# Query weights in one set of chunks, converted with the key weights in slots 9 to 12 of the last unit of a head group

## The chip, the cores and the metric

One core of a Trainium2 chip runs the whole program. The metric is the device time of one execution in microseconds (us). A difference of about 0.3% (8 us here) is what a measurement of this kernel can tell from none.

## What is computed

A decoder layer on x of 16 sequences x 256 tokens x 512 features, in float32. The change touches only the first of its three parts, the self-attention with 16 heads of size 128:

```python
q = split_heads(hidden_states @ wq)
k = split_heads(hidden_states @ wk)
v = split_heads(hidden_states @ wv)
...
q = _apply_rotary(q, cos, sin)
k = _apply_rotary(k, cos, sin)
...
attn = jnp.einsum('bhqd,bhkd->bhqk', q, k) * scale
attn = jnp.where(valid, attn, neg)
attn = jax.nn.softmax(attn, axis=-1)
out = jnp.einsum('bhqk,bhkd->bhqd', attn, v)
...
return out @ wo
```

After it come a cross-attention with a context and a mixture of experts.

## The kernel before

**Units and slots.** The 16 heads are four head groups of four heads (g = 0 to 3), and the 16 sequences are eight pairs. A unit u is one pair in one group: 32 units, u = 8g + pair, one after the other. A unit has 16 slots (the code's `s`; k is `s % SLOTS`), and in each slot TensorE does one projection of 12 matmuls of 128x512. The table `FRAME` says which: in slots 0 to 3 the values (V) of the unit, in 4 and 8 the queries (Q) of its heads 2 and 3, in 5 and 9 the keys (K) of its heads 2 and 3, in 6, 7, 10 and 11 the output projection (O) of the unit before, and in 12 to 15 Q0, K0, Q1, K1 of the next unit. Even slots begin with the scores of a head (lines 572 to 575), odd slots with the transposes of probabilities (583) and their product with V (594, 595). Every engine runs the same slots in its own program order; only semaphores hold one for another.

**Weights in two parts.** A weight chunk is 128x512 of float32; each of Q, K, V and O has four chunks per group. Each chunk is loaded by SyncE's DMA queue into one of four buffers `raw` (`load_raw`, line 274), rounded by ScalarE to `whi` (`w_round`, 728), and the rest, raw less whi, is taken by GpSimd into `wlo` (`w_rest`, 442). A projection of a kind waits until all four chunks of that kind are there (`weights_at`, a count on the semaphore `s_wlo`). `sequence` numbers the chunks; chunk i may be loaded only when chunk i - 4 has been through GpSimd (`s_wlo` at i - 3). `converted(s)` says which chunks go through in slot s, and SyncE, ScalarE and GpSimd all read it in their own loops over s. `last_use` is what `w_round` waits for before it writes over a chunk of the group before.

**The change of head group.** It falls into units 7, 15 and 23, called here changes 1, 2 and 3. There, before: Q chunks of the next group in slots 0 to 3, V chunks in 4 to 7, K chunks two and two in slots 10 and 11. Q has two sets of chunks (0 to 3 and 16 to 19), so its new weights can be written while the old are in use. The first user of the new Q weights is the projection in slot 12, of the new K weights the one in slot 13.

**SyncE's queue in such a unit.** In program order: the loads of `converted(s)`; at slot 10 also `load_xn(u + 2)` (line 260: two DMAs of 1024 KB, the normalised input of two units on), which waits until the K projection of slot 9 is done; at slot 12 the store and the load of the residual rows (291, 286).

**ScalarE in slots 10 to 13 of such a unit**: the exponentials of step 5 (`exps`, 709), the roundings of that slot (728), `pt_evac` (716), the roundings of slot 11, two `o_round` (722), the exponentials of slot 12, `pt_evac`. VectorE takes the row maxima (871) in slot 12 only after the rest of the first rounded output (`o_rest`, 885), and the product with V in slot 13 (594) waits for that rest too. GpSimd adds the two halves of the rotary turn (`turn_add`, 435) one slot after each Q or K projection, ahead of the `w_rest` of its slot.

Of the kernel before, what the change touches and what calls it, by code (L numbers as in the profile page):

```python
# [6 lines left out]
F32R = mybir.dt.float32r  # L7
# [6 lines left out]
P = 128  # L14
B, L, D = 16, 256, 512
TILES = B * L // P
TB = L // P
CB = D // P
# [4 lines left out]
NCH = 3 * CB + HG  # L23
# [9 lines left out]
CH_Q, CH_K, CH_V, CH_O = 0, CB, 2 * CB, 3 * CB  # L33


def attention_stages(nc, x, w_all, rope, xt, x1, ctx_in, ctx_t, gamma, sq, sk, mv2, mv3, x2, x2_at, cst):
# [4 lines left out]
    with ctx:  # L41
# [38 lines left out]
        def at(name, shape, dt, kb):  # L80
            return nc.alloc_sbuf_tensor_at(name, shape, dt, offset=area + int(kb * KB))
# [25 lines left out]
        var2 = at("var2", [P, TILES], F32, 27.5)  # L107
        seed2 = at("seed2", [P, TILES], I32, 27.75)
        half2 = at("half2", [P, TILES], F32, 28)
        STACK_AT = (0, CH_V, CH_K)  # L110
        qst = [at(f"qst{i}", [P, XPT, D], F32R, 60.5 + 2 * STACK_AT[i]) for i in range(STACKS)]
        kst = [at(f"kst{i}", [P, XPT, D], F32R, 100.5 + 2 * STACK_AT[i]) for i in range(STACKS)]
        qp = [at(f"qp{i}", [P, 2, D], F32R, 60.5 + 2 * NCH + 4 * i) for i in range(2)]
        kp = [at(f"kp{i}", [P, 2, D], F32R, 100.5 + 2 * NCH + 4 * i) for i in range(2)]
        RING_AT = (60.5 + 2 * CH_O, 100.5 + 2 * CH_O, 28.5, 36.5, 44.5, 52.5)
        xprt = [at(f"xprt{i}", [P, XPT, D], F32, RING_AT[i]) for i in range(RING)]

# [45 lines left out]
        PAIRS = B // 2  # L163
# [8 lines left out]
        at, turned, number, place, order = {}, {}, {}, {}, []  # L172
# [10 lines left out]
        for s in range(FIRST, LAST):  # L183
            kind, ahead, i = FRAME[s % SLOTS]
# [7 lines left out]

        def sequence(g, kind, c):

            return NCH * g + 4 * ("QVKO" if g else "QKVO").index(kind) + c

        def weights_at(g, kind):

            return sequence(g, kind, 3) + 1

        def chunk_of(g, kind, c):

            if kind == "Q":
                return (16 if g % 2 else 0) + c
            return {"K": CH_K, "V": CH_V, "O": CH_O}[kind] + c

        def converted(s):

            f, k = s // SLOTS, s % SLOTS
            g = (f + 1) // PAIRS  # L210
            if f % PAIRS == PAIRS - 1 and 0 < g < G:
                if k < 4:
                    return [(g, "Q", k)]
                if k < 8:
                    return [(g, "V", k - 4)]
                if k in (10, 11):
                    return [(g, "K", 2 * (k - 10) + i) for i in range(2)]
            g = f // PAIRS
            if f % PAIRS == 0 and 0 <= g < G and k >= 12:
                return [(g, "O", k - 12)]  # L220
            return []
# [2 lines left out]

        def last_use(g, kind):

            if kind == "Q":
                return number["K", PAIRS * (g - 1) - 1, 3] if g > 1 else 0
            u = PAIRS * g - 1
            return number[kind, u, 3] + 1 if g else 0  # L230

# [24 lines left out]
        def _(sp):  # L256
# [10 lines left out]
            def load_raw(g, kind, c):  # L267
                i = sequence(g, kind, c)
                if i >= 4:
                    sp.wait_ge(s_wlo, i - 3)  # L270
                if i in (3 * CB, NCH):
                    sp.wait_ge(s_nrm, 8 if i < NCH else 4 * PAIRS)
                src = w_all[g, {"Q": CH_Q, "K": CH_K, "V": CH_V, "O": CH_O}[kind] + c]
                sp.dma_start(raw[:, i % 4, :], src).then_inc(s_raw[i % 4], 16)
# [75 lines left out]
            for s in range(0, LAST + 1):  # L350
                u, k = s // SLOTS, s % SLOTS
                for part in converted(s):
                    load_raw(*part)
# [56 lines left out]
        def _(pool):  # L410
# [27 lines left out]
            def w_rest(g, kind, c):  # L438
                i = sequence(g, kind, c)
                pool.wait_ge(s_whi, i + 1)  # L440
                n = chunk_of(g, kind, c)
                nc.gpsimd.tensor_tensor(wlo[:, n, :], raw[:, i % 4, :], whi[:, n, :].bitcast(F32),
                                        ALU.subtract).then_inc(s_wlo, 1)
# [30 lines left out]
            for s in range(-3, LAST + 1):  # L474
                if s - 1 in at and at[s - 1][0] in "QK":
                    turn_add(*at[s - 1])
                if s < 1:
                    w_rest(*FIRST_WEIGHTS[11 + s])
                for part in converted(s):
                    w_rest(*part)  # L480
                if s == TAIL + 7:
                    nc.gpsimd.memset(xones[:, :], 1.0).then_inc(c_ones, 1)
                    pool.wait_ge(c_ones, 1)
                    pool.wait_ge(s_blk, number["V", LASTU, 3] + 1)
                    row_of_ones(0)
                    row_of_ones(1)
                if s in (TAIL + 10, TAIL + 12, TAIL + 14):
                    q_rest((s - TAIL - 10) // 2)
                    k_rest((s - TAIL - 10) // 2)
                if s == TAIL + 15:  # L490
                    pool.wait_ge(s_blk, number["K", LASTU, 3] + 1)
                    pool.wait_ge(c_klo, 3)
                    row_of_ones(2)
# [14 lines left out]
        def _(pe):  # L508
# [14 lines left out]
            def projection(kind, u, i):  # L523
                n, g = number[kind, u, i], u // PAIRS
                bank, xn = PJ[n % 3], xnt[u % 2]
                if u < PAIRS:
                    pe.wait_ge(s_llo, 4 * u + 4)
                else:
                    pe.wait_ge(s_xn[u % 2], 32 * ((u - PAIRS) // 2 + 1))
                pe.wait_ge(s_wlo, weights_at(g, kind))  # L530
                bank_free(n)
                k = 0
                for c in range(CB):
                    w = chunk_of(g, kind, c)
                    for xpart, wpart in ((0, whi), (0, wlo), (1, whi)):
                        moving = xn[:, xpart, c, :, :].rearrange("p b n -> p (b n)")
                        if kind == "V":
                            last = nc.tensor.matmul(bank[:, :], moving[:, i * P:(i + 1) * P], wpart[:, w, :],  # L538
                                                    start=(k == 0), stop=(k == 3 * CB - 1))
                        else:  # L540
                            last = nc.tensor.matmul(bank[:, :], wpart[:, w, i * HD:(i + 1) * HD], moving,  # L541
                                                    start=(k == 0), stop=(k == 3 * CB - 1))
                        k += 1
                last.then_inc(s_blk, 1)
# [148 lines left out]
        def _(act):  # L693
# [30 lines left out]
            def w_round(g, kind, c):  # L724
                i = sequence(g, kind, c)
                act.wait_ge(s_raw[i % 4], 16 * (i // 4 + 1))
                act.wait_ge(s_blk, last_use(g, kind))
                nc.scalar.activation(whi[:, chunk_of(g, kind, c), :], raw[:, i % 4, :], ACT.Copy).then_inc(s_whi, 1)
# [712 lines left out]
def decoder_layer(nc, x, ctx_in, ctx_t, w_all, gamma, router_w, router_b, expert_w, expert_b, rope, out):  # L1441
    xt = nc.dram_tensor("xt_scratch", [B, P, 2, CB, L], F32).ap()
    x1 = nc.dram_tensor("x1_scratch", [B, P, TB, D], F32).ap()
    sq = nc.dram_tensor("sq_scratch", [2, 2, P, D], F32).ap()
    sk = nc.dram_tensor("sk_scratch", [2, 2, P, D], F32).ap()
    ctx = ExitStack()
    with ctx:
        def sb(name, shape, dt):
            return ctx.enter_context(nc.sbuf_tensor(name, shape, dt))

        cst = dict(ident=sb("ident", [P, P], F32), identb=sb("identb", [P, P], BF16), mask=sb("mask", [P, P], BF16),
                   ones=sb("ones", [P, P], BF16), tri=sb("tri", [P, P], BF16))
        mv2 = sb("mv2", [P, TILES, 2], F32)
        mv3 = sb("mv3", [P, TILES, 2], F32)
        x2_at = -(-nc.sbuf_base // 32) * 32
        x2 = sb("x2", [P, TILES, D], F32)
        attention_stages(nc, x, w_all, rope, xt, x1, ctx_in, ctx_t, gamma, sq, sk, mv2, mv3, x2, x2_at, cst)
        expert_mix(nc, router_w, router_b, expert_w, expert_b, mv3, x2, out, cst)
# [39 lines left out]
```

## Time and profile before

| | before |
|---|---|
| time, median of 3 runs | 2697.91 us (2694.23 to 2702.70) |
| time of the profiled execution | 2697.19 us |
| its span, first to last instruction | 2695.4 us |
| TensorE busy | 95% |
| VectorE / ScalarE / GpSimd busy | 66% / 36% / 32% |
| mean granted TensorE clock | 0.981 |

The profile is of one execution. Busy time of TensorE counts overlapping matmuls once; what matters below is where it is idle and what ended the idle time. A clock of 1.00 in a row is 2.4 GHz, 0.50 is 1.2 GHz.

### The profile page before, as it was taken

The numbers are of one execution on the slowest core, as the hardware profiler recorded it, in microseconds if no ns is written. First come the engines' busy times: TensorE is split into PE (matmuls) and PEld (weight loads), VectorE is DVE, ScalarE is ACT, GpSimd is POOL, SyncE is SP. The second block draws the span as 40 slices with busy tenths as digits, with TensorE's granted clock in tenths as the row PEclk, the third lists the DMA queues.
The fourth block names the chain that finished last, engine by engine and source line by source line (L and its number), as shares of the span: only waits on it lengthen the run. The fifth ranks groups of instructions, "written<-read, shape, count | busy, mean of one in ns | idle before, by whom it ended". The sixth has DMA issues, their size and how long they took to land. (4 is left out here: it accounts for less than half of the span.)

```text
span 2695.4 us, 37398 instructions
## 1 busy us (share of the span) xinstructions
PE 2571.5 (95%) x12936; PEld 1916.8 (71%) x12936; DVE 1786.7 (66%) x3722; ACT 965.5 (36%) x2434; POOL 861.9 (32%) x698
## 2 busy tenths in 40 slices
PE   6999999999999999999999999999879999999794
PEld 5888888888888888888887888888644444443673
DVE  5777776565656555565665566666677888876657
ACT  2322223322222232222223322222347777776220
POOL 3211111321111232111113211112248888887000
PEclk9999999999999999999999999999989999999897
DMA  3122233221222222112222211221356666662003
GB/s 117 63 79 94 98 121 118 86 79 63 83 89 79 82 91 79 63 64 101 87 79 94 79 63 63 78 95 71 105 185 194 222 220 218 221 221 72 21 1 125
DMA packets 170152, 280.61 MB, mean 104 GB/s; under 512 B 15088, under 2 KB 81648, under 8 KB 169968
## 3 DMA queue, kind: packets, MB, share of 16 engines
q1 hardware_dynamic: 169968, 278.23, 30.9%
q8 instruction: 107, 1.75, 0.3%
q14 instruction: 77, 0.63, 0.1%
HBM read 185.37 MB, written 92.27 MB: 103 GB/s over the span
## 5 line engine op out<-in xcount | busy, mean ns | idle before, releaser
L541 PE MATMUL pj<-xnt,whi 128*128 128x512 f32 x2048 | 706.9, 407 | 5.9 <-DVE xnt L926 5.9
L709 ACT ACTIVATE pr<-sc,nmx 128x128 f32<-128x128 f32 (+1 forms) x512 | 210.6, 416 | 930.1 <-DVE nmx L871 930.1
L435 POOL TENSOR_TENSOR qt<-rot,swp 128x512 f32<-128x512 f32 x128 | 165.9, 1296 | 1107.9 <-DVE swp L851 1098.5
L541 PEld LDWEIGHTS pj<-xnt,whi 128*128 128x128 f32 x2048 | 387.7, 189 | 99.1 <-DVE xnt L926 6.8
L541 PE MATMUL pj<-xnt,wlo 128*128 128x512 f32 x1024 | 400.4, 391 | 0.0
L538 PE MATMUL pj<-whi,xnt 128*128 128x512 f32 x1024 | 352.9, 406 | 4.0 <-issue 4.0
L461 POOL TENSOR_TENSOR xprt<-xprt,xprt 128x512 f32<-128x512 f32 x256 | 320.6, 1284 | 82.1 <-PE ob L630 82.1
L766 ACT ACTIVATE xprt<-pj 128x512 f32<-128x512 f32 x512 | 290.8, 595 | 142.4 <-PE pj L619 140.9
L849 DVE TENSOR_TENSOR rot<-pj,trig 128x512 f32<-128x512 f32 x256 | 176.5, 690 | 212.4 <-PE pj L541 212.4
L955 DVE TENSOR_REDUCE xnmx<-sc 128x1 f32<-128x512 f32 x342 | 227.2, 680 | 70.9 <-PE sc L608 70.5
L435 POOL TENSOR_TENSOR kt<-rot,swp 128x512 f32<-128x512 f32 x128 | 164.8, 1288 | 308.2 <-DVE swp L851 308.2
L880 DVE TENSOR_SCALAR pr<-pr,rinv 128x128 f32<-128x128 f32 (+1 forms) x512 | 255.5, 540 | 9.0
L871 DVE TENSOR_REDUCE nmx<-sc 128x1 f32<-128x128 f32 (+1 forms) x512 | 158.3, 351 | 146.8 <-PE sc L575 142.3
L538 PEld LDWEIGHTS pj<-whi,xnt 128*128 128x128 f32 x1024 | 193.4, 189 | 50.4 <-issue 4.3
L619 PE MATMUL pj<-qst,kst 98*128 98x512 f32 x512 | 211.0, 414 | 13.3 <-DMA qst<-xmlo 10.4
L541 PEld LDWEIGHTS pj<-xnt,wlo 128*128 128x128 f32 x1024 | 195.0, 190 | 34.6
L562 PE MATMUL pj<-whi,ohi 128*128 128x512 f32 x512 | 213.6, 417 | 0.0
L562 PE MATMUL pj<-whi,olo 128*128 128x512 f32 x512 | 202.3, 395 | 0.0
L859 DVE TENSOR_TENSOR xio<-pj,xio 128x512 f32<-128x512 f32 x128 | 88.4, 691 | 169.4 <-PE pj L562 169.4
L562 PE MATMUL pj<-wlo,ohi 128*128 128x512 f32 x512 | 200.3, 391 | 0.0
L538 PE MATMUL pj<-wlo,xnt 128*128 128x512 f32 x512 | 199.8, 390 | 0.0
L850 DVE TENSOR_TENSOR swp<-pj,trig 64x512 f32<-64x512 f32 x256 | 177.3, 692 | 3.4
(185 smaller groups left out, 4296.9 us busy)
## 6 DMA issues: line engine op xcount, KB each, us to landing
xnt<-xt_scratch SPq DMA_DIRECT2D x48, 1024.0 KB, 7.3
x_scratch<-xio SPq DMA_DIRECT2D x64, 512.0 KB, 3.6
xio<-x_scratch SPq DMA_DIRECT2D x48, 512.0 KB, 4.1
qst<-sq_scratch SPq DMA_DIRECT2D x192, 128.0 KB, 2.6
kst<-sk_scratch SPq DMA_DIRECT2D x192, 128.0 KB, 2.6
raw<-in_w_all_dram SPq DMA_DIRECT2D x64, 256.0 KB, 4.6
xt_scratch<-xnt SPq DMA_DIRECT2D x16, 1024.0 KB, 8.5
sq_scratch<-qp SPq DMA_DIRECT2D x32, 512.0 KB, 3.4
```

What stands on the lines that cost most here:

```text
L435: nc.gpsimd.tensor_tensor(qk["QK".index(kind)][h][:, :, :].rearrange("p b n -> p (b n)"), rot[r % 2][:, :], swp[r % 2][:, :], ALU.add).the ...
L461: nc.gpsimd.tensor_tensor(a[:, h, :], a[:, h, :], b[:, h, :], ALU.add).then_inc(c_add, 1)
L538: last = nc.tensor.matmul(bank[:, :], moving[:, i * P:(i + 1) * P], wpart[:, w, :], start=(k == 0), stop=(k == 3 * CB - 1))
L541: last = nc.tensor.matmul(bank[:, :], wpart[:, w, i * HD:(i + 1) * HD], moving, start=(k == 0), stop=(k == 3 * CB - 1))
L562: last = nc.tensor.matmul(PJ[n % 3][:, :], o[:, h, tok], w[:, CH_O + h, :], start=(h == 0 and k == 0), stop=(h == HG - 1 and k == 2))
L619: nc.tensor.matmul(XST[h % 2][:, :], kst[n % STACKS][0:KM, h, c * P:(c + 1) * P], qst[n % STACKS][0:KM, h, :], start=True, stop=True).then ...
L709: nc.scalar.activation(pr[:, a % 4, lo:hi], SC[a % 2][:, lo:hi], ACT.Exp, bias=nmx[:, a % 4, t:t + 1], accum_out=rsum[:, a % 4, t:t + 1]). ...
L766: nc.scalar.activation(xprt[s % RING][:, h, :], XST[h % 2][:, :], ACT.Exp).then_inc(c_exp, 1)
L849: nc.vector.tensor_tensor(ro, bank, table(slice(0, P), q), ALU.mult)
L850: nc.vector.tensor_tensor(sw[top], bank[low], table(low, q + 1), ALU.mult)
L880: nc.vector.tensor_scalar(pr[:, a % 4, lo:hi], pr[:, a % 4, lo:hi], rinv[:, a % 4, t:t + 1], None, ALU.mult).then_inc(s_pr, 1)
L955: nc.vector.tensor_reduce(xnmx[:, m % 2, k:k + 1], XSC[(4 * g + q) % 3][:, :], AX.X, ALU.max, negate=True).then_inc(c_mx, 1)
```

## The change

Q gets one set of chunks, 0 to 3; chunks 16 to 19 of the same buffers are then unused in the self-attention, and the first stack of the cross-attention (`qst`, `kst`) lies there, while the query and context parts `qp` and `kp` lie in chunks 0 to 3. At a change of head group the chunks are numbered V, Q, K, O and go through so: V in slots 4 to 7 as before, then Q0, Q1, Q2 in slot 9, Q3 and K0 in slot 10, K1 and K2 in slot 11, K3 in slot 12. The new Q weights now wait for the last Q projection of the old group (slot 8), through the general rule of `last_use`.

```diff
-        STACK_AT = (0, CH_V, CH_K)
+        STACK_AT = (NCH, CH_V, CH_K)
...
-        qp = [at(f"qp{i}", [P, 2, D], F32R, 60.5 + 2 * NCH + 4 * i) for i in range(2)]
-        kp = [at(f"kp{i}", [P, 2, D], F32R, 100.5 + 2 * NCH + 4 * i) for i in range(2)]
+        qp = [at(f"qp{i}", [P, 2, D], F32R, 60.5 + 2 * CH_Q + 4 * i) for i in range(2)]
+        kp = [at(f"kp{i}", [P, 2, D], F32R, 100.5 + 2 * CH_Q + 4 * i) for i in range(2)]
...
         def sequence(g, kind, c):
 
-            return NCH * g + 4 * ("QVKO" if g else "QKVO").index(kind) + c
+            return NCH * g + 4 * ("VQKO" if g else "QKVO").index(kind) + c
...
         def chunk_of(g, kind, c):
 
-            if kind == "Q":
-                return (16 if g % 2 else 0) + c
-            return {"K": CH_K, "V": CH_V, "O": CH_O}[kind] + c
+            return {"Q": CH_Q, "K": CH_K, "V": CH_V, "O": CH_O}[kind] + c
+
+        QK_PARTS = [(kind, c) for kind in "QK" for c in range(CB)]
+        QK_AT = ((0, 1, 2), (3, 4), (5, 6), (7,))
 
         def converted(s):
 
             f, k = s // SLOTS, s % SLOTS
             g = (f + 1) // PAIRS
             if f % PAIRS == PAIRS - 1 and 0 < g < G:
-                if k < 4:
-                    return [(g, "Q", k)]
-                if k < 8:
+                if 4 <= k < 8:
                     return [(g, "V", k - 4)]
-                if k in (10, 11):
-                    return [(g, "K", 2 * (k - 10) + i) for i in range(2)]
+                if 9 <= k < 13:
+                    return [(g, *QK_PARTS[i]) for i in QK_AT[k - 9]]
...
         def last_use(g, kind):
 
-            if kind == "Q":
-                return number["K", PAIRS * (g - 1) - 1, 3] if g > 1 else 0
             u = PAIRS * g - 1
             return number[kind, u, 3] + 1 if g else 0
```

SyncE's queue at change 1, before. The rows are loads into `raw`, the two loads `xnt` of `load_xn`, and the store and load of residual rows (`xio`):

```order
36 L274 DMA raw_49<-in_w_all_dram 128x512 x10
37 L260 DMA xnt_71<-xt_scratch 128x8x256 x2
38 L274 DMA raw_49<-in_w_all_dram 128x512 x2
39 L291 DMA x_scratch<-xio 128x1024 x2
40 L286 DMA xio<-in_x_dram 128x2x512 x2
```

The same place in the changed kernel (its line numbers are three lower):

```order
36 L271 DMA raw_49<-in_w_all_dram 128x512 x9
37 L257 DMA xnt_71<-xt_scratch 128x8x256 x2
38 L271 DMA raw_49<-in_w_all_dram 128x512 x3
39 L288 DMA x_scratch<-xio 128x1024 x2
40 L283 DMA xio<-in_x_dram 128x2x512 x2
```

Nine loads (V, Q, K0) now stand ahead of the two large ones and three (K1, K2, K3) behind, where it was ten (Q, V, K0, K1) and two (K2, K3).

ScalarE at change 1, before, from the exponentials of slot 8 to `pt_evac` of slot 13 (`pr` exponentials, `whi` rounding of weights, `prt` `pt_evac`, `ohi` `o_round`):

```order
282 L709 ACTIVATE pr,rsum<-sc,nmx 128x128
283 L709 ACTIVATE pr,rsum<-sc,nmx 128x256
284 L716 ACTIVATE prt_68<-tr 128x384
285 L709 ACTIVATE pr,rsum<-sc,nmx 128x128
286 L709 ACTIVATE pr,rsum<-sc,nmx 128x256
287 L728 ACTIVATE whi<-raw_49 128x512 x2
288 L716 ACTIVATE prt_65<-tr 128x384
289 L728 ACTIVATE whi<-raw_49 128x512 x2
290 L722 ACTIVATE ohi<-ob 128x512 x2
291 L709 ACTIVATE pr,rsum<-sc,nmx 128x128
292 L709 ACTIVATE pr,rsum<-sc,nmx 128x256
293 L716 ACTIVATE prt_66<-tr 128x384
```

The changed kernel over the same slots:

```order
281 L725 ACTIVATE whi<-raw_49 128x512 x3
282 L706 ACTIVATE pr,rsum<-sc,nmx 128x128
283 L706 ACTIVATE pr,rsum<-sc,nmx 128x256
284 L725 ACTIVATE whi<-raw_49 128x512 x2
285 L713 ACTIVATE prt_65<-tr 128x384
286 L725 ACTIVATE whi<-raw_49 128x512 x2
287 L719 ACTIVATE ohi<-ob 128x512 x2
288 L706 ACTIVATE pr,rsum<-sc,nmx 128x128
289 L706 ACTIVATE pr,rsum<-sc,nmx 128x256
290 L725 ACTIVATE whi<-raw_49 128x512
291 L713 ACTIVATE prt_66<-tr 128x384
```

Three roundings (Q0 to Q2) now stand in slot 9, and one (K3) behind the exponentials of slot 12; the last rounding of K stood ahead of the two `o_round` before.

GpSimd at change 1, before, slots 6 to 13 (`qt` and `kt` are `turn_add`, `wlo` is `w_rest`):

```order
89 L442 TENSOR_TENSOR wlo<-raw_49,whi 128x512 x2
90 L435 TENSOR_TENSOR qt_59<-rot_52,swp_54 128x512
91 L435 TENSOR_TENSOR kt_63<-rot_53,swp_55 128x512
92 L442 TENSOR_TENSOR wlo<-raw_49,whi 128x512 x4
93 L435 TENSOR_TENSOR qt_56<-rot_52,swp_54 128x512
```

And in the changed kernel:

```order
89 L439 TENSOR_TENSOR wlo<-raw_49,whi 128x512 x2
90 L432 TENSOR_TENSOR qt_59<-rot_52,swp_54 128x512
91 L439 TENSOR_TENSOR wlo<-raw_49,whi 128x512 x3
92 L432 TENSOR_TENSOR kt_63<-rot_53,swp_55 128x512
93 L439 TENSOR_TENSOR wlo<-raw_49,whi 128x512 x5
94 L432 TENSOR_TENSOR qt_56<-rot_52,swp_54 128x512
```

Three rests of Q chunks now stand between the last two `turn_add` of the old group, and five rests instead of four behind them.

## Rows read from the trace of the kernel before

**Rows 1.** The page, part 1: busy us, share of the span, instructions.

```profile
PE 2571.5 (95%) x12936; PEld 1916.8 (71%) x12936; DVE 1786.7 (66%) x3722; ACT 965.5 (36%) x2434; POOL 861.9 (32%) x698
```

**Rows 2.** Waits of TensorE, 0 to 1750 us: total us, times, longest.

```profile
PE pj L551 <- DVE xn L920: 12.1, 2, 11.8
...
PE ob L594 <- DVE olo L885: 4.4, 3, 2.1
```

**Rows 3.** Windows: length, busy us of PE, PEld, DVE, ACT, POOL; clock, DMA share, GB/s.

```profile
450.00:497.76 47.76, 47.76 (x240) 39.52 (x239) 30.00 (x59) 16.09 (x45) 19.38 (x15) 1.00 0.39 124
497.76:513.00 15.24, 14.49 (x73) 11.81 (x72) 10.55 (x19) 5.86 (x16) 7.05 (x6) 1.00 0.77 269
972.00:988.00 16.00, 14.40 (x73) 11.75 (x72) 10.47 (x19) 5.86 (x16) 6.89 (x6) 1.00 0.77 261
...
1448.00:1465.00 17.00, 14.95 (x67) 12.07 (x66) 10.98 (x20) 5.86 (x16) 7.61 (x6) 0.90 0.79 273
```

**Rows 4.** Timeline of SyncE at change 1: start, us, what, count.

```profile
453.77 30.50 SPq L274 DMA_DIRECT2D raw<-in_w_all_dram  x10
497.76 1.29 SPq L260 DMA_DIRECT2D xnt<-xt_scratch  x2
499.09 2.17 SPq L274 DMA_DIRECT2D raw<-in_w_all_dram  x2
```

**Rows 5.** Issue to landing: K0, K1 before load_xn; load_xn; K2, K3 behind it.

```profile
DMA to landing us min/median/max: 2.6/2.6/2.7
DMA to landing us min/median/max: 5.8/7.0/8.2
DMA to landing us min/median/max: 7.0/7.6/8.1
```

**Rows 6.** Timeline of ScalarE, change 1, slots 11 to 13; then changes 2 and 3.

```profile
507.23 1.26 ACT L728 ACTIVATE whi<-raw 128x512 fp32r<-128x512 f32 x2 [4.35 <-DMA raw<-in_w_all_dram]
508.40 1.06 ACT L722 ACTIVATE ohi<-ob 128x512 fp32r<-128x512 f32 x2
510.26 0.37 ACT L709 ACTIVATE pr<-sc,nmx 128x128 f32<-128x128 f32 x1 [0.80 <-DVE nmx L871]
511.07 0.49 ACT L716 ACTIVATE prt<-tr 128x384 f32<-128x384 f32 x1
...
982.34 1.27 ACT L728 ACTIVATE whi<-raw 128x512 fp32r<-128x512 f32 x2 [5.18 <-DMA raw<-in_w_all_dram]
...
1458.33 1.28 ACT L728 ACTIVATE whi<-raw 128x512 fp32r<-128x512 f32 x2 [5.63 <-DMA raw<-in_w_all_dram]
```

**Rows 7.** Timeline of GpSimd at change 1, slots 9 to 12.

```profile
496.19 1.30 POOL L435 TENSOR_TENSOR qt<-rot,swp 128x512 f32<-128x512 f32 x1 [5.33 <-DVE swp L851]
499.94 1.29 POOL L435 TENSOR_TENSOR kt<-rot,swp 128x512 f32<-128x512 f32 x1 [2.45 <-DVE swp L851]
...
507.94 2.52 POOL L442 TENSOR_TENSOR wlo<-raw,whi 128x512 fp32r<-128x512 f32 x2 [3.34 <-ACT whi L728]
```

**Rows 8.** Timeline of TensorE: slots 12 and 13 of change 1; slot 13 of changes 2 and 3.

```profile
505.75 0.47 PE L541 MATMUL pj<-xnt,whi 128*128 128x512 f32 x1
...
509.84 0.67 PE L594 MATMUL ob<-prt,v 128*128 128x256 f32 x2 [0.75 <-DVE olo L885]
510.55 0.47 PE L541 MATMUL pj<-xnt,whi 128*128 128x512 f32 x1
...
984.97 0.67 PE L594 MATMUL ob<-prt,v 128*128 128x256 f32 x2 [1.60 <-DVE olo L885]
985.65 0.47 PE L541 MATMUL pj<-xnt,whi 128*128 128x512 f32 x1
...
1460.96 0.67 PE L594 MATMUL ob<-prt,v 128*128 128x256 f32 x2 [2.05 <-DVE olo L885]
1461.63 0.76 PE L541 MATMUL pj<-xnt,whi 128*128 128x512 f32 x1
```

**Rows 9.** Windows, the stretch after the wait of change 3 (clock behind the counts).

```profile
1461.63:1465.05 3.42, 3.42 (x11) 2.77 (x10) 3.32 (x7) 1.04 (x5) 1.28 (x1) 0.50 0.77 286
```

## The prediction

> **What bounds the kernel now.** I read the page first: TensorE is busy 2571.5 us of a span of 2695.4 [rows 1]. Then its waits up to 1750 us, the self-attention, where the change lies. Beside the start-up (the two waits of 12.1 us in all) one group matters: the product with V (line 594) waited three times for `olo`, 4.4 us in all, 2.1 the longest [rows 2]. The windows place these: TensorE is busy 14.49 of 15.24 us at change 1, 14.40 of 16.00 at change 2 and 14.95 of 17.00 at change 3, so idle 0.75, 1.60 and 2.05, and in the 47.76 us of slots before change 1 not at all [rows 3]. So in the self-attention TensorE sets the time slot by slot: any further wait of it is added to the time in full, and work that ScalarE, VectorE or GpSimd is spared in slots 0 to 8 gains nothing, there being no idle time to win.
>
> Why it waits at a change is seen in the next views. SyncE issues ten weight loads, then `load_xn` at 497.76 (after the K projection of slot 9), then K2 and K3 at 499.09 and just after [rows 4]. A weight load alone lands in 2.6 us; the two large loads need 5.8 and 8.2 us, and K2 and K3 behind them 8.1 and 7.0 [rows 5]. ScalarE, standing at the rounding of K2 in slot 11, idles 4.35 us for it, to 507.23; at changes 2 and 3 it is 5.18 and 5.63 us, to 982.34 and 1458.33 [rows 6]. Queued behind that rounding are K3's rounding, the two `o_round` at 508.40, and so VectorE's `o_rest`, for which TensorE's product at 509.84 waits, and the row maxima, for which ScalarE's exponentials at 510.26 wait [rows 6, 8]. The K weights are ready by 507.94 + 2.52 = 510.46 [rows 7], and the first new K projection starts at 510.55 [rows 8]. It hardly waits itself. I count all that follows from ScalarE's start on the first chunk behind `load_xn`, called A: 507.23, 982.34 and 1458.33. The K projection starts at 510.55, 985.65 and 1461.63 [rows 8], that is A + 3.3 each time.
>
> **What moves, and what it costs.** The instructions are the same in number; the extra cost is all in order.
>
> Slots 0 to 3: four Q chunks leave. By the idle time above, the gain is 0.
>
> Slots 9 and 10, Q: its first two loads can go when V0's and V1's rests are done, as K0's and K1's do now, within the 30.50 us of the ten loads, by 484.3 [rows 4], so the data wait in `raw` for slot 9. The `turn_add` of Q3 ends at 496.19 + 1.30 = 497.49; a `wlo` is 2.52 / 2 = 1.26, with its start some 1.27 after the last. So Q0, Q1, Q2 end at 498.8, 500.05 and 501.3. The `turn_add` of K3, at 499.94 now [rows 7], starts 1.4 us later and ends at 502.6, Q3 ends at 503.9. The Q projection of slot 12 starts at 505.75 [rows 8]: 1.8 us in hand, the same hides the late `turn_add` (its reader stands in the scores of slot 12, some 0.8 us earlier). If this cover were gone and Q came up to 4 us late, the K projection behind it, which waits for longer by the sum below, would hide most of that. I take 0.
>
> Slot 10, SyncE: K0's load is now ninth, and needs the buffer that Q0's rest frees at 498.8. It stands ahead of `load_xn`, which thus goes at about 499.2 and not at 497.76 [rows 4]: 1.4 us later. K0's 256 KB also run ahead of it. K2 and K3 were back to back and landed at 499.09 + 8.1 = 507.2 and some 0.65 later, so 0.65 is the most that K0 adds, 0 the least; I take 0.4, since K0 is issued hardly ahead. K1 is now the first chunk behind `load_xn`. A moves by 1.4 + 0.4 = 1.8 us (bounds 1.4 and 2.1).
>
> Slot 12, K3: from A on, ScalarE does what it did: two roundings, two `o_round`, the exponentials after VectorE's maxima, to 511.07 [rows 6], which is A + 3.84. Before, the last K chunk was already through. Now K3's rounding only starts here. GpSimd starts 507.94 - 507.23 = 0.71 after a rounding starts and takes 1.26 to 1.3 [rows 6, 7]. So the K weights are whole at A + 3.84 + 0.71 + 1.28 = A + 5.83, and with 0.1 to TensorE's start (510.46 to 510.55) the K projection starts at A + 5.9 instead of A + 3.3: 2.6 us. K3 has landed by then: its load needs Q3's rest, at 503.9, and comes in behind K2, near 510.5 against a need at 512.9.
>
> Queued behind K3's rounding on ScalarE is `pt_evac` of slot 13, at 511.07 now [rows 6], 0.6 us later; TensorE wants its result two slots on, behind the K projection, which is itself late. What is late next is only what stands behind the K projection on TensorE, everything by the same amount.
>
> Sum of a change: 1.8 + 2.6 = 4.4 us. At change 1: A = 509.0, product with V at 511.6, K projection at 514.9 against 510.55. Three changes: 13.2 us.
>
> **The clock.** At change 3 the clock is 0.90 over the stretch [rows 3]: just after the wait of 2.05 us it is 0.50, 1.2 GHz, for 3.42 us with TensorE busy throughout [rows 9], which costs half, 1.7 us. At changes 1 and 2, after waits of 0.75 and 1.60, it stays at 1.00 [rows 3]. After the change each has an idle time of 0.75 to 2.05 plus 4.4, 5.2 to 6.5 us, broken only by the product with V. I expect the half clock after all three, at 1.7 us each as in rows 9: 5.1, less the 1.7 paid now, 3.4. Bounds: 0 (the fall is spent inside the idle time, or none more) and 7 (each stays down for double).
>
> The Trainium skill ("TensorE: Matmul & The Clock Gate", the part on the clock gate) says that an idle array falls to half rate and comes back after sustained work. By that rule too the stall costs more than its own length, and this speaks against the change; the fall at change 3 agrees with it.
>
> **Sum against the profile's own time**: 2697.2 + 13.2 + 3.4 = 2713.8, which is 16.6 us or 0.6% more. The profiled execution is 0.7 us under the median of the runs shown, so I predict 2714.
>
> **Rivals.**
>
> *The small loads overtake the large ones* (not slower). If K1 to K3 landed in 2.6 us from their issue, near 503.4, 504 and 506.6, ScalarE would not stand still in slot 11, K3's rounding would follow the exponentials of slot 12 at about 507, and its rest end near 508.5, before the 509.1 at which an undisturbed slot 13 wants it. The waits of today would go too: 0.75 + 1.60 + 2.05 and the 1.7 of clock, 6 us: 2691. It decides where A + 5.9 falls under 509.8, A under 504. Against it: K2 and K3, in the same place today, landed after `load_xn` all three times [rows 5, 6]. I give it 3%.
>
> The Trainium skill ("DMA: Bandwidth & Descriptors", the section on queues, rings and completion order) says that completion is not in order per issuing engine. That would allow this rival; the rows here show no such case.
>
> *Only the new place of K3 costs.* `load_xn` has its time from its own traffic, K0 costs it nothing and the 1.4 us are made good, the clock adds nothing: 3 x 2.6 = 7.8 us, 2705, on the edge of what can be told from no change. For it: the landing times behind `load_xn` differ by over 1 us between the changes (waits 4.35 to 5.63 [rows 6]). Against it: the 1.4 us is a plain chain through one buffer. 12%, half of it under 0.3%.
>
> *The stall is longer than its chain.* Q also late beyond the cover, K1 and K2 delayed by their issue, the half clock for double: 2 more us a change and 5 of clock, some 25 us: 2722 and above. 10%.
>
> *The change does not act at run time*, the wait of the product with V covering all. Then 2698. It would need K whole by A + 3.3, while K3 is not even rounded. 2%, with other ways to no change 4%.
>
> The forecast, K whole at A + 5.9 with A 1.4 to 2.1 later and some clock loss, has the other 70%.
>
> **How the numbers follow.** The forecast's own range is 3 x (1.4 + 2.6) + 0 = 12 to 3 x (2.1 + 2.6) + 7 = 21, that is 2710 to 2719, and with the runs' scatter of some 4 us 2707 to 2722. The second rival's end takes the low side to 2706, which leaves out under 2 in 10. About 8 us, 0.3%, can be told from nothing: slower by more than that is the forecast's 70%, the longer stall's 10%, half of the 12% and a little, 0.87. Within it 0.10, faster 0.03.
>
> **What the changed profile would show.** Right: TensorE waits in slot 13 of each change twice, for `olo` before line 591 and for the K weights (a rest by GpSimd) before the K projection, together 5 to 6.5 us; ScalarE's wait for `raw` in slot 11 ending 1.4 to 2.1 us later, and so about 6 us long where it was 4.35 to 5.63; `load_xn` issued at about 499.2; a GpSimd row of three `wlo` before `kt`; clock 0.50 after each change. Wrong, if TensorE has idle time in slots 9 to 12 (Q late), if A does not move, if K3's rounding stands before the exponentials, or if `raw` loads land before `xnt`.

## The result, and the profile after

The changed kernel takes 2719.64 us (median of 4 runs, 2716.8 to 2724.3) against 2698.71 for the kernel before (4 runs, 2694.23 to 2702.7). The ratio is 1.0075, with a 95% interval of 1.006 to 1.009: 0.75% slower. One later execution of the changed kernel took 3072 us at a mean clock of 0.792, where every other execution of this case lies between 2690 and 2726 us; it is left out of all comparisons here.

The profiled execution of the changed kernel took 2724.3 us, the longest of its four; its span is 2722.6. TensorE's waits up to 1750 us (who, for whom, total, times, longest), where [rows 2] had 4.4 us for `olo`:

```profile
PE pj L548 <- DVE xn L917: 11.9, 2, 11.6
PE ob L591 <- DVE olo L882: 11.3, 3, 3.9
PE pj L538 <- DVE xnt L923: 6.7, 2, 6.1
PE pj L538 <- issue: 5.6, 3, 2.2
PE sc L569 <- POOL kt L432: 4.0, 3, 1.9
```

Two groups have grown: the product with V waits 11.3 us for `olo`, and the K projection behind it another 5.6. That second wait is put down to "issue"; what it follows is GpSimd's last `wlo`, as the timelines below show. Together 16.9 where it was 4.4. TensorE's rows in slot 13 of the three changes, which answer to [rows 8]:

```profile
514.67 1.19 PE L591 MATMUL ob<-prt,v 128*128 128x256 f32 x2 [3.61 <-DVE olo L882]
...
517.97 0.76 PE L538 MATMUL pj<-xnt,whi 128*128 128x512 f32 x1 [1.68 <-issue]
...
997.60 0.67 PE L591 MATMUL ob<-prt,v 128*128 128x256 f32 x2 [3.74 <-DVE olo L882]
...
1000.90 0.77 PE L538 MATMUL pj<-xnt,whi 128*128 128x512 f32 x1 [2.22 <-issue]
...
1479.44 1.19 PE L591 MATMUL ob<-prt,v 128*128 128x256 f32 x2 [3.93 <-DVE olo L882]
...
1482.74 0.77 PE L538 MATMUL pj<-xnt,whi 128*128 128x512 f32 x1 [1.68 <-issue]
```

SyncE at change 1, against [rows 4]: K0's load alone, the two large loads, then K1 to K3:

```profile
500.72 0.33 SPq L271 DMA_DIRECT2D raw<-in_w_all_dram  x1
501.15 1.29 SPq L257 DMA_DIRECT2D xnt<-xt_scratch  x2
502.48 4.25 SPq L271 DMA_DIRECT2D raw<-in_w_all_dram  x3
```

ScalarE at change 1, against [rows 6]:

```profile
504.34 1.15 ACT L725 ACTIVATE whi<-raw 128x512 fp32r<-128x512 f32 x2
505.38 0.49 ACT L713 ACTIVATE prt<-tr 128x384 f32<-128x384 f32 x1
512.04 1.28 ACT L725 ACTIVATE whi<-raw 128x512 fp32r<-128x512 f32 x2 [6.17 <-DMA raw<-in_w_all_dram]
513.23 1.07 ACT L719 ACTIVATE ohi<-ob 128x512 fp32r<-128x512 f32 x2
515.09 0.37 ACT L706 ACTIVATE pr<-sc,nmx 128x128 f32<-128x128 f32 x1 [0.80 <-DVE nmx L868]
...
515.90 0.62 ACT L725 ACTIVATE whi<-raw 128x512 fp32r<-128x512 f32 x1
```

GpSimd, against [rows 7]; the row of 516.60 is K3's rest:

```profile
498.16 1.30 POOL L432 TENSOR_TENSOR qt<-rot,swp 128x512 f32<-128x512 f32 x1 [5.33 <-DVE swp L848]
499.42 3.82 POOL L439 TENSOR_TENSOR wlo<-raw,whi 128x512 fp32r<-128x512 f32 x3
503.20 1.28 POOL L432 TENSOR_TENSOR kt<-rot,swp 128x512 f32<-128x512 f32 x1
505.05 2.57 POOL L439 TENSOR_TENSOR wlo<-raw,whi 128x512 fp32r<-128x512 f32 x2 [0.57 <-ACT whi L725]
512.75 2.49 POOL L439 TENSOR_TENSOR wlo<-raw,whi 128x512 fp32r<-128x512 f32 x2 [5.13 <-ACT whi L725]
516.60 1.27 POOL L439 TENSOR_TENSOR wlo<-raw,whi 128x512 fp32r<-128x512 f32 x1 [1.36 <-ACT whi L725]
```

This execution reaches the `qt` sum of Q3 at 498.16, not at 496.19 [rows 7]: it is 1.97 us behind before the first change, from the start-up (the first 120 us), and that is to be taken off when times of change 1 are compared. K3's rounding starts behind the exponentials at 515.90, its rest ends at 516.60 + 1.27 = 517.87, and the K projection starts at 517.97. At change 1 it starts 517.97 - 1.97 = 516.0, where it was 510.55.

The windows from slot 10 to past the stall, at changes 1, 2 and 3 (columns as in [rows 3]), and the three stretches at half clock inside them:

```profile
499.70:525.00 25.30, 20.01 (x83) 15.90 (x83) 12.82 (x24) 6.38 (x17) 12.34 (x10) 0.80 0.61 207
...
982.50:1006.00 23.50, 17.54 (x78) 14.00 (x78) 11.46 (x22) 6.38 (x17) 12.33 (x10) 0.85 0.64 224
1464.10:1487.00 22.90, 17.29 (x75) 13.77 (x74) 11.35 (x21) 6.38 (x17) 12.42 (x10) 0.85 0.66 230
...
513.48:523.72 10.24, 7.37 (x19) 5.73 (x20) 5.77 (x11) 2.63 (x8) 4.26 (x4) 0.50 0.34 113
998.17:1005.00 6.83, 4.61 (x13) 3.48 (x12) 4.11 (x7) 1.67 (x6) 2.50 (x2) 0.50 0.42 155
1479.45:1486.28 6.83, 5.15 (x12) 3.98 (x13) 4.67 (x9) 1.81 (x6) 2.50 (x2) 0.50 0.44 160
```

Idle TensorE: 25.30 - 20.01 = 5.29, 5.96 and 5.61 us, all of it the two waits of slot 13. The half clock begins before the K projection, at change 1 at 513.48, inside the wait for `olo`. At half clock it was busy 7.37 + 4.61 + 5.15 = 17.1 us, of which half, 8.6, is lost, against 1.7 before. The `qt` sums of Q3 before change 1 (496.19 before [rows 7], 498.16 after) and at the end of the last unit enclose all three changes:

```profile
1926.53 1.29 POOL L435 TENSOR_TENSOR qt<-rot,swp 128x512 f32<-128x512 f32 x1 [9.46 <-issue]
```

in the kernel before, and in the changed kernel

```profile
1947.67 1.29 POOL L432 TENSOR_TENSOR qt<-rot,swp 128x512 f32<-128x512 f32 x1 [9.45 <-issue]
```

That is 1430.34 and 1449.51 us: 19.2 us are lost between them, by the count 16.9 - 4.4 = 12.5 of idle time and 8.6 - 1.7 = 6.9 of half clock. The rest of the 27.1 us between the two profiled executions is 2.0 at the start and some 6 after the last of these sums. I read that as the scatter of single executions: this last part takes 769 to 777 us in the four profiles with one set of Q chunks and 769 to 776 in the six with two. The medians differ by 20.9.

### The profile page after: what moved, and what is told of

It reads as the page before. It is cut to its first block and busy times, and to the rows that moved or that the text cites. A ratio compares the mean times of both kernels' runs of the same rounds, so it can differ in the third digit from the quotient of the medians.

```text
span 2722.6 us, 37398 instructions
## 1 busy us (share of the span) xinstructions
PE 2581.2 (95%) x12936; PEld 1922.2 (71%) x12936; DVE 1787.4 (66%) x3722; ACT 966.5 (35%) x2434; POOL 861.0 (32%) x698
## 5 line engine op out<-in xcount | busy, mean ns | idle before, releaser
L616 PE MATMUL pj<-qst,kst 98*128 98x512 f32 x512 | 212.3, 417 | 17.6 <-DMA qst<-xmlo 15.3
```

Source lines behind the costliest of these rows:

```text
L616: nc.tensor.matmul(XST[h % 2][:, :], kst[n % STACKS][0:KM, h, c * P:(c + 1) * P], qst[n % STACKS][0:KM, h, :], start=True, stop=True).then ...
```

## The experiments

Each was timed beside the kernel before on the same chip, in two groups. In the first (before 2701.72 us) were the order with two sets of Q chunks, the large loads in slot 12 in both kernels, and K3 in slot 11. In the second (before 2702.12 us) were the changed kernel again, the order with two sets again, K3 in slot 12 in the kernel before, and the large loads issued later. Each difference is taken to the median of its own group.

### The order with two sets of Q chunks

```diff
-            return {"Q": CH_Q, "K": CH_K, "V": CH_V, "O": CH_O}[kind] + c
+            if kind == "Q":
+                return (16 if g % 2 else 0) + c
+            return {"K": CH_K, "V": CH_V, "O": CH_O}[kind] + c
...
+            if kind == "Q":
+                return number["K", PAIRS * (g - 1) - 1, 3] if g > 1 else 0
```

The stacks and `qp`, `kp` lie as in the kernel before; the rest is the changed kernel's.

> The changed order of conversions, but with two sets of Q chunks, the old last_use for Q and the stacks of the cross-attention where they lay before. Theory order (all of the loss is the order of loads and roundings at the three changes): as the changed kernel, some 21 us over before, waits of TensorE in slot 13 of 5.3 to 6 us. Theory storage (writing the new Q chunks over the old ones, or the moved stacks, cost a wait): clearly less than the changed kernel.

Measured 2716.36 us, ratio 1.0056 (1.0044 to 1.0068): 14.6 us over before, where some 21 were expected, with 13.4 us of waits in slot 13, 4.2 to 4.8 a change, where 5.3 to 6 were. The intervals of this and of the changed kernel overlap, so the order makes most of the loss, but 3 us between the medians of different groups left the storage open. The pair was therefore repeated on one chip:

> The changed kernel as it is, a second time. In its first profile ScalarE started on K1 10.6 to 10.9 us after the issue of the two large loads; before it was 9.5 to 10.75, and 9.6 to 10.6 in the two other kernels that keep its queue order. Theory scatter (the transfers behind each other take 9.5 to 10.9 us by chance of the execution): here anywhere in that span, and the time between 2715 and 2720. Rival storage (single set of Q chunks makes the landing later): again 10.6 or more, and slower than the run with two sets beside it by 3 us or more.

> The changed order with two sets of Q chunks, beside the changed kernel on the same chip. Theory scatter: the same as the changed kernel within 2 us. Rival storage: 3 us or more under it, as between the first runs (ratios to before 1.0056 and 1.0075).

The changed kernel took 2719.62 us (median of 5 runs; ratio 1.0069, 1.0052 to 1.0085), the one with two sets 2718.56 (6 runs; 1.0061, 1.0046 to 1.0076): 1.1 us apart, with intervals that nearly coincide. In this second profile of the changed kernel ScalarE started on K1 at 511.36, the large loads being issued at 501.92: 9.4 us behind, where the first profile had 10.9 (512.04 and 501.15):

```profile
511.36 1.31 ACT L725 ACTIVATE whi<-raw 128x512 fp32r<-128x512 f32 x2 [4.71 <-DMA raw<-in_w_all_dram]
```

With two sets the waits of TensorE in slot 13 are 8.3 for `olo` and 5.8 before the K projection, with one set in the second profile 8.3 and 5.9. And up to the large loads the queues run alike: they are issued 2.97 to 2.99 us after the start of the `qt` sum of Q3 in every change of all four profiles. So no wait is seen that storage could have made, and the difference in time is within the intervals. It is not shown to be nothing: between the two `qt` sums the two profiles with one set lost 19.2 and 17.9 us, the two with two sets 15.4 and 15.3. What differs there is the landing behind the large loads and the length at half clock, which also differ between two executions of one kernel.

### The two large loads issued in slot 12

```diff
-                if k == 10 and PAIRS <= u + 2 < UNITS:
+                if k == (12 if u % PAIRS == PAIRS - 1 else 10) and PAIRS <= u + 2 < UNITS:
```

In the changed kernel:

> The changed kernel, but at a change of group SyncE issues the two large loads of the normalised input after K3's load in slot 12, not in slot 10. Theory large loads (K1 to K3 stand behind 2 MB in the queue, and that is what ScalarE waits for): ScalarE's wait of 6 us in slot 11 goes, TensorE's waits in slot 13 fall under 0.5 us, no half clock after the changes: 2691 to 2694, so under before. Theory work (the eight roundings and rests in slots 9 to 12 are too much for ScalarE or GpSimd): waits of 2 us and more stay, time over before.

Measured 2696.79 us, ratio 0.9983 (0.9973 to 0.9992): 4.9 us under before. The 2691 to 2694 that was expected, 4 to 7 under the 2698 of the first measurement, is met as a difference and not as a time. SyncE's queue and ScalarE at change 1 (this execution is 1.6 us ahead of the kernel before there):

```profile
497.18 6.02 SPq L271 DMA_DIRECT2D raw<-in_w_all_dram  x4
503.29 1.29 SPq L257 DMA_DIRECT2D xnt<-xt_scratch  x2
...
503.64 1.09 ACT L719 ACTIVATE ohi<-ob 128x512 fp32r<-128x512 f32 x2 [0.28 <-PE pj L559]
505.53 0.37 ACT L706 ACTIVATE pr<-sc,nmx 128x128 f32<-128x128 f32 x1 [0.80 <-DVE nmx L868]
...
506.34 0.63 ACT L725 ACTIVATE whi<-raw 128x512 fp32r<-128x512 f32 x1
```

No rounding waits for `raw`, nothing waits for `olo`, and K3's rounding, still behind the exponentials, leaves TensorE 0.24 us of wait at each change (0.7 in all). The same roundings and rests in the same four slots cost under 1 us when the large loads are out of their way. The theory of too much work falls.

In the kernel before:

> The kernel before with the same late issue of the two large loads at a change of group. Theory large loads: the three waits of TensorE before the product with V (0.75, 1.60, 2.05 us) and the half clock after the third (1.7) go: 6 us under before, 2692. If the waits come from anything else, no difference.

Measured 2695.65 us, ratio 0.9976 (0.9965 to 0.9987): 6.1 us less, as worked out. Its list of TensorE's waits holds the start-up and no more, but for 0.2 us:

```profile
PE pj L551 <- DVE xn L920: 11.7, 2, 11.4
PE pj L541 <- DVE xnt L926: 6.8, 2, 6.2
PE pj L538 <- issue: 4.0, 1, 4.0
PE sc L572 <- POOL kt L435: 3.9, 3, 1.9
```

This is the fastest version found, ahead of both kernels; its lead over the changed kernel with the same edit, 1.1 us, is not clear.

### K3 in slot 11

```diff
-        QK_AT = ((0, 1, 2), (3, 4), (5, 6), (7,))
+        QK_AT = ((0, 1, 2), (3, 4), (5, 6, 7))
...
-                if 9 <= k < 13:
+                if 9 <= k < 12:
```

> The changed kernel with K3 rounded in slot 11 with K1 and K2, ahead of the two roundings of the output, instead of behind the exponentials of slot 12. Theory chain (K weights are whole at A + 5.9, A being ScalarE's start on the first chunk behind the large loads, because K3 stands behind the exponentials): the product with V comes 0.6 us later and the K projection at about A + 4.6, so 1.3 us less stall a change, 4 us less than the changed kernel plus some of the half clock, 2714 to 2716. Rival (only the landing counts, K3's place nothing): same as the changed kernel.

Measured 2711.20 us, ratio 1.0038 (1.0023 to 1.0052): 9.5 us over before instead of 17.5 to 21. That is a gain of 8 to 11 us on the changed kernel, more than the 4 to 6 that was expected, and 3 us under the time given. At change 1, ScalarE (A = 507.27) and TensorE:

```profile
507.27 1.95 ACT L725 ACTIVATE whi<-raw 128x512 fp32r<-128x512 f32 x3 [4.87 <-DMA raw<-in_w_all_dram]
...
510.57 0.67 PE L591 MATMUL ob<-prt,v 128*128 128x256 f32 x2 [2.96 <-DVE olo L882]
...
511.79 0.76 PE L538 MATMUL pj<-xnt,whi 128*128 128x512 f32 x1 [0.33 <-issue]
```

The K projection starts at A + 4.5, as said (4.6), and the product with V at A + 3.3, 0.7 later behind A than before (509.84 - 507.23). The idle time of the three changes is 10.8 + 0.3 = 11.1 us, 5.8 less than in the first profile of the changed kernel and 3.1 less than in its second. The rest of the gain is clock: 4.3 us of half clock over before (table below), where the two profiles of the changed kernel have 6.9 and 7.6.

### K3 in slot 12, in the kernel before

```diff
-                if k in (10, 11):
-                    return [(g, "K", 2 * (k - 10) + i) for i in range(2)]
+                if k in (10, 11, 12):
+                    return [(g, "K", c) for c in ((0,), (1, 2), (3,))[k - 10]]
```

> The kernel before with K0 in slot 10, K1 and K2 in slot 11 and K3 in slot 12, so with the changed kernel's place of K3 alone: Q stays in slots 0 to 3 and K0's load is not late, the two large loads go as early as before. Theory chain: A (ScalarE's start on K1) as before, the K projection at A + 5.9 instead of A + 3.3, so 2.6 us more idle time a change (3.3, 4.2 and 4.6 in all), 7.8 us, and 2 to 5 us of half clock: 10 to 13 us over before. Rival (K3's place is hidden behind the wait for A): as before.

Measured 2714.87 us, ratio 1.0048 (1.0034 to 1.0063): 12.8 us. At change 1, ScalarE and TensorE:

```profile
508.63 1.31 ACT L728 ACTIVATE whi<-raw 128x512 fp32r<-128x512 f32 x2 [4.80 <-DMA raw<-in_w_all_dram]
...
512.52 0.62 ACT L728 ACTIVATE whi<-raw 128x512 fp32r<-128x512 f32 x1
...
511.30 0.67 PE L594 MATMUL ob<-prt,v 128*128 128x256 f32 x2 [0.74 <-DVE olo L885]
...
514.59 0.74 PE L541 MATMUL pj<-xnt,whi 128*128 128x512 f32 x1 [2.40 <-issue]
```

The wait for `olo` is as in the kernel before (4.3 us in all), and a second one of 2.4 us stands behind it three times (7.2): the K projection at 514.59 - 508.63 = A + 5.96. The term of K3 is shown alone: 7.2 us of idle time, and 5.6 us of the measured 12.8 on top. Counted in its trace, the half clock after the three changes costs 5.7 us over before.

### The two large loads 3.5 us later, in the kernel before

```diff
                     sp.wait_ge(s_blk, number["K", u, 3] + 1)
+                    if u % PAIRS == PAIRS - 1:
+                        sp.wait_ge(s_rot, place["K", u, 3] + 1)
```

> The kernel before, where the two large loads at a change also wait for the last rotary sum of the old group (GpSimd, ends near 501.2 at change 1), some 3.5 us later than now. Theory: A moves by the same 3.5 us, and all of it appears as idle time before the product with V: 4.2, 5.1 and 5.5 us, the K projection still at A + 3.3; 10.5 us and 3 to 5 of half clock, 13 to 16 us over before. If the landing of the large loads were hidden or set by other traffic, less.

Measured 2713.29 us, ratio 1.0046 (1.003 to 1.0062): 11.2 us, 2 under the range. The issue at change 1 (this execution is 1.2 us ahead of the kernel before there), and TensorE's waits for `olo`:

```profile
500.09 1.29 SPq L260 DMA_DIRECT2D xnt<-xt_scratch  x2
...
PE ob L596 <- DVE olo L887: 14.2, 3, 5.5
```

That is 9.8 us more than before, 3.3 a change, for an issue 3.5 us later (500.09 + 1.2 against 497.76): the time at which the large loads are issued passes through to TensorE almost in full, in one wait, with none before the K projection.

## Why the prediction was right

2714 was forecast with a range of 2706 to 2722, and 2719.6 measured. Direction, place and mechanism held; two sizes were off, and by luck in opposite directions: the idle time was a little smaller than summed, the half clock twice as large. The measured 20.9 us lie at the upper end of the 12 to 21 that the sum itself allowed.

*What bounds.* Right: the loss lies in slot 13 of the three units. The large loads in front of K chunks are what ScalarE waits for, shown by taking them away in both kernels.

*Slots 0 to 3, a gain of 0.* Right as far as the runs can tell. With the large loads out of the way the changed order is no faster than the old one (2696.79 against 2695.65 us), so its emptier slots 0 to 3 gain nothing.

*Q in slots 9 and 10, 0.* Right: the Q projection of slot 12 shows no wait. The cover is thinner than said. Q3's rest ends near 505.05 + 1.29 = 506.3, not at 503.9 + 1.97 = 505.9, because slot 10's exponentials came later (last section).

*A moves by 1.8 us (1.4 to 2.1).* The chain through the buffer was right: the large loads were issued at 501.15 - 1.97 = 499.2, as said. What follows the issue was not the fixed time that I made of it. In the first profile A moved by 512.04 - 1.97 - 507.23 = 2.8 us at change 1, over my bound; in the second, whose `qt` sum there stands at 498.95 and so 2.76 behind, by 1.4. At changes 2 and 3 it was 1.9 and 1.3 us in the first and 1.8 and 0.6 in the second, 1.6 on average over the six. From issue to ScalarE's start it took from 9.4 to 10.9 us in the 24 changes of eight profiles. With K0 in front the mean is 10.2 (15 changes), without it 10.1 (9 changes), so the 0.4 us that I took for K0's traffic is hardly seen. A bound for a transfer must hold the scatter of its landing, which [rows 6] had shown (waits of 4.35 to 5.63) and which I used for a rival only.

*K3 behind the exponentials, 2.6 us a change.* Right to 0.1 at change 1: A + 5.93 in the first profile (517.97 - 512.04), A + 5.96 with K3's place alone, A + 4.5 with K3 in slot 11. At changes 2 and 3 of the first profile it was A + 6.2 and A + 6.6, because ScalarE waited once more, 0.25 and 0.64 us, for K2's own load; in the other four profiles with K3 in slot 12 behind the large loads it was A + 5.9 to A + 6.0 every time.

*The idle time, 13.2 us.* It was 12.5 in the first profile; in the second 8.3 + 5.9 - 4.4 = 9.8.

*The clock, 3.4 us.* This term was mis-sized: 6.9 in the first profile and 7.6 in the second. I let each change cost what one stretch of 3.42 us at half clock had cost [rows 9]. Measured were 10.24, 6.83 and 6.83 us at 0.50, and TensorE was busy in most of each. The loss is at the bound of 7 that I gave, under it once and over it once; its 3.5 us and more over the 3.4 of the forecast are the larger part of the 5.6 us between forecast and median. The Trainium skill ("TensorE: Matmul & The Clock Gate", the part on the clock gate) says that the array returns to full rate only after sustained work. The rows agree: with the waits of slot 13 over and TensorE at work again, at change 1 the clock stays at 0.50 to 523.72, 5.75 us after the K projection starts.

That idle time and half clock are the whole loss can be counted in every profile, between the `qt` sum of Q3 before change 1 and the last one of the self-attention. Half clock is half of TensorE's busy time in the stretches at 0.50 after the three changes. All figures are us over the kernel before; the last column is of the medians, the others of one execution each.

| | idle | half clock | lost between the sums | medians |
|---|---|---|---|---|
| changed kernel | 12.4 | 6.9 | 19.2 | 20.9 |
| changed kernel, again | 10.4 | 7.6 | 17.9 | 17.5 |
| its order, two sets | 9.5 | 5.6 | 15.4 | 14.6 |
| its order, two sets, again | 9.5 | 5.6 | 15.3 | 16.4 |
| its order, K3 in slot 11 | 6.5 | 4.3 | 10.3 | 9.5 |
| before, K3 in slot 12 | 6.9 | 5.7 | 12.8 | 12.8 |
| before, large loads 3.5 us later | 9.5 | 5.0 | 14.0 | 11.2 |
| changed kernel, large loads in slot 12 | -3.9 | -1.7 | -5.6 | -4.9 |
| before, large loads in slot 12 | -4.4 | -1.7 | -6.5 | -6.1 |

The two sum to the loss within about 0.5 us in each.

*The rivals.* The small loads never overtook the large: wherever K chunks stood behind the large loads, in 24 changes of eight profiles, they landed behind them, the first by 0.6 to 1.8 us. K3's place alone was to give 2705; it gives 2714.87 - 2702.12 = 12.8 over before, because it too brings the clock down. So the lowest case of the forecast was too cheap for the same reason.

Not settled: how a given idle time sets the length at half clock. 9.5 us more of idle time cost 5.0 us of half clock in one piece a change (large loads later) and 5.6 broken in two (the order with two sets), and 6.9 us cost 5.7. The changed kernel's own two profiles have 6.9 and 7.6 for 12.4 and 10.4. So the half clock does not simply grow with the idle time, and no rule for it comes out of these runs.

## What to carry to other kernels

Where a small load is wanted soon, put it ahead of the large one that is wanted late, in the queue that both share; here one condition on the slot of 2 MB of loads brings both orders under the kernel before, by 6.1 and 4.9 us, which no placing of the small ones tried here did. When a count on one semaphore releases a whole kind of work, its price is that of the last piece: follow that piece through every in-order engine, and look at what stands ahead of it in the last slot. And price a stall of TensorE at its length plus the half clock behind it, which was from a third to a half of the loss in every slower kernel here (table above).

## What the runs showed of the hardware

VectorE's multiplication of the probabilities (line 880 before, 877 after), from SBUF to SBUF, does not end before a GpSimd operation that was running when it started. Slot 9's pair at change 1, before and after (min, median, max in ns; the shorter is the 128x256 one before, the longer the 128x256 one after):

```profile
L880 DVE TENSOR_SCALAR pr<-pr,rinv x2: 344/784/1225, 496.3 to 497.5; 128x128 f32<-128x128 f32 x1, 128x256 f32<-128x256 f32 x1
```

```profile
L877 DVE TENSOR_SCALAR pr<-pr,rinv x2: 1227/1304/1380, 498.3 to 499.5; 128x128 f32<-128x128 f32 x1, 128x256 f32<-128x256 f32 x1
```

The 128x256 piece takes 0.34 us alone and 1.38 us beside the first of the three `wlo` that the change puts there (499.42), so all that VectorE does after it, and with it the exponentials of slot 10 and Q3's and K0's rounding, comes 1.0 us later. It was off the path here. It is no single case: in the trace of the kernel before, up to 1750 us, all 130 of these pieces that start while GpSimd is at work end 0.08 to 0.16 us after its operation, while those that start beside an idle GpSimd take 0.29 us (128x128) and 0.34 to 0.35 us (128x256). The Trainium skill ("SBUF — State Buffer", "Who interferes with whom") says that VectorE's `tensor_scalar` can take the port pair that it shares with GpSimd, and that the one that comes second then blocks for the whole instruction. The trace agrees: the piece starts 0.04 us after `wlo` and ends at 500.84, 0.15 after it.
